# A two-layer transformer kernel: the eight row scatters of two batches, four in a row and two couples before, are given eight release points spread over two batches

## The chip, the cores and the metric

One core of a Trainium2 chip runs the whole program. The metric is device time in microseconds (us), lower is better. Engines are named as in the profile: PE is TensorE (matmul and transpose), DVE is VectorE, ACT is ScalarE, POOL is GpSimd, SP is SyncE, which here only issues transfers.

## The reference

Two transformer layers work on 32 batches of 256 rows of 128 features.

```
x  = L0_attn_x                                   # 32 x 256 x 128
xn = layernorm(x)
x  = x + attention0(xn) + moe0(xn)                # 16 heads, relative position bias clipped at 64
xn = layernorm(x)
x  = x + attention1(xn) + moe1(xn)                # ALiBi, causal; 16 experts with a capacity

# inside moe1
logits = xn @ router_w.T + router_b
vals, idx = top_k(logits, 2)
pos  = running count of each expert's rows        # in row order
slot = idx * capacity + pos                       # rows over the capacity are dropped
buf  = zeros(16 * capacity + 1, 128).at[slot].set(each row, twice)
h    = gelu(buf @ w1 + b1) @ w2 + b2              # then gathered back and weighted
```

The change concerns the line `buf = ... .at[slot].set(...)`: each normalized row is written twice, into the slots of its two experts. In the kernel `buf` is the DRAM tensor `packed`.

## The kernel before

The program has four stages one after the other: the first mixture of experts (0 to about 440 us of the trace), the first attention (about 440 to 1650), the second mixture's experts (to about 1945), and the second attention. The change is in the first attention.

The first attention takes the batches one by one, with eight steps for each batch (`UB = 8`): a step is 128 query rows times four heads. Step n belongs to batch b = n // 8 and has place r = n % 8; this document writes r0 to r7. In a step the four engines work on different ages of the data, by orders written out by hand:

- PE computes `score(n+1)` and `relative(n+5)` (lines 1172 and 1182), transposes the probabilities of step n-2 (`turn`, line 1194), and multiplies them with the values of step n-3 (line 1214) and with the relative table (lines 1229 and 1159). `score(n+1)` may start only when DVE has read the scores of step n (the semaphore `lowest`) and has copied the relative part (`rel_moved`).
- DVE adds scores and bias and takes the minimum, four instructions in a step (line 1013, tile `neg_scores`), each of which raises `lowest` by one; then it copies the relative part (`rel_s`, line 1021) and does small work that depends on r.
- ACT takes the exponentials (line 873) and moves the transposed probabilities out of PSUM (lines 889, 895).
- SP issues the transfers of the relative bias, a write to and a read from DRAM in each step (lines 764, 777).
- POOL makes the heads of the queries of the next batch (`query_heads`, line 825, or 828 for the later batches), and issues the scatters.

As soon as two batches of the first attention are complete, their 512 rows (a pair p, four tiles of 128 rows) are normalized, routed and counted, by small DVE work in the steps of the batches 2p+3 to 2p+5. In r5 of the odd batch b = 2p+5 DVE finishes the slots (`slots`, last instruction on line 985, semaphore `slots_done`). POOL then makes the row numbers (`rows_of(p)`, lines 816 and 818) and issues eight indirect DMAs, for each of the four tiles one to the first and one to the second expert (line 844). Each writes 128 rows of 512 bytes into `packed`. Sixteen pairs make 128 scatters. Batches 32 to 35 of this stage are already those of the second attention (ALiBi instead of the relative bias, shorter steps); the pairs 13, 14 and 15 are scattered at batches 31, 33 and 35.

A scatter has a release point: POOL waits until `lowest` has reached four times a step number, that is, until DVE has read all scores before that step. Before the change the eight of a pair wait, two by two, for the steps 8b+6, 8b+7, 8b+8 and 8b+9, capped at step 256 (`NU0`), beyond which no pacing exists. POOL works strictly in its order: what stands behind a scatter waits with it. Two things wait for the scatters to land: `rows_of(p+1)` (the list `scat` is reused) and the DVE normalization of pair p+2 (`normal_end`, r7 of an odd batch; the tile `xn2` is reused).

Of the kernel before, what the change touches and what calls it, by code (L numbers as in the profile page):

```python
# [61 lines left out]
def program(nc, io, nb, cap):  # L62
# [5 lines left out]
    with ctx:  # L68
# [7 lines left out]
        packed = nc.dram_tensor("packed", (SLOTS + 2 * T, D), F32).ap()  # L76
# [38 lines left out]
        with ExitStack() as pa:  # L115
# [10 lines left out]
            TP = 4  # L126
# [468 lines left out]
        with ExitStack() as pm:  # L595
# [9 lines left out]
            TP = 4  # L605
            UB = 8
            NU0 = UB * nb
            NB0 = nb + LATE
            NUL = UB * NB0
# [25 lines left out]
            xn2 = [sm(f"xn2_{i}", [P, TP, D]) for i in range(2)]  # L635
# [26 lines left out]
            scat = sm("scat", [P, TP, 2], U32)  # L662
# [12 lines left out]
            lowest = semm("lowest_ready")  # L675
# [18 lines left out]
            scattered = semm("scattered")  # L694
# [27 lines left out]
            for s in range(0, UB * (NB0 + 2)):  # L722
                b, r = divmod(s, UB)
                odd = b % 2 == 1
# [83 lines left out]
            @block.gpsimd  # L808
            def _(pool):
                for i in range(3):  # L810
                    pool.memset(bias[0][i][:, :, :], 0.0).then_inc(bias_zeroed, 1)
                def rows_of(p):
                    pool.wait_ge(slots_done, p + 1)
                    if p >= 1:
                        pool.wait_ge(scattered, 128 * p)
                    pool.tensor_tensor(scat_f[:, :, :], dumpk[:, :, :], sk[:, :, :], ALU.add).then_inc(rows_known, 1)
                    pool.wait_ge(rows_known, 2 * p + 1)
                    pool.tensor_copy(scat[:, :, :], scat_f[:, :, :]).then_inc(rows_known, 1)
                    pool.wait_ge(rows_known, 2 * p + 2)

                def query_heads(b):
                    pool.wait_ge(spare_free, job_no["q", b])
                    for i in range(4):
                        if b < nb:
                            ins = pool.tensor_scalar(q_of[b % 2][:, i, :], q_raw[:, :], cview["head_scale"][:, i:i + 1], q_bias[:, i:i + 1],  # L825
                                                     ALU.mult, ALU.add)
                        else:
                            ins = pool.tensor_scalar(q_of[b % 2][:, i, :], q_raw[:, :], cview["head_scale"][:, i:i + 1], None, ALU.mult)
                    ins.then_inc(q_ready, 1)

                query_heads(0)
                for b in range(nb + 5):
                    if b + 1 < NB0:
                        query_heads(b + 1)
                    if b == 2:
                        for h in range(H):
                            pool.tensor_scalar(alibi[:, h, :], cview["distance"], float(SLOPES[h]), None, ALU.mult).then_inc(alibi_built, 1)
                    p, odd = divmod(b - 5, 2)
                    if odd == 0 and 0 <= p < nb // 2:
                        rows_of(p)  # L840
                        for i in range(TP):
                            for k in range(2):
                                pool.wait_ge(lowest, 4 * min(NU0, UB * b + 6 + i))
                                pool.indirect_dma_start(
                                    out=packed, out_offset=bass.IndirectOffsetOnAxis(ap=scat[:, i, k:k + 1], axis=0),
                                    in_=xn2[p % 2][:, i, :], in_offset=None).then_inc(scattered, 16)
                pool.wait_ge(scattered, 128 * (nb // 2))

            @block.scalar
# [686 lines left out]
        with ExitStack() as pb:  # L1536
# [38 lines left out]
            lowest = semb("lowest_ready")  # L1575
# [16 lines left out]
            UB = 8  # L1592
# [353 lines left out]
```

## Time and profile before

| | |
|---|---|
| device time, three runs | 2600.22 us median (2595.81 to 2603.77) |
| the profiled execution | 2601.3 us, of which the span of the trace is 2599.2 us |
| busy share over the span | PE 87%, PEld (weight loads) 69%, DVE 74%, ACT 66%, POOL 32% |
| granted TensorE clock, mean | 0.951 |
| the 128 scatters (line 844) | 953 / 967 / 1207 ns on POOL (min / median / max), 625.9 to 1637.5 us |
| from a scatter's issue to its landing | 3.8 / 4.0 / 15.7 us |

All times are those of one profiled execution, counted from the span's start. The shares are averages over four stages with different limits; for this change the reader has to look at single steps of the first attention. In rows of the timeline the first number is the start, the second the duration, and the bracket at the end says how long the engine stood idle before the instruction and what released it; "issue" stands for an idle time in which the engine waited for nothing that the profile shows. Such a bracket is absent where the idle time was very short.

### The profile page before, as it was taken

To read this page: it belongs to the slowest core of one execution; us is meant where nothing else is said; L and a number is where in the kernel's file an instruction comes from. 1 tells how busy PE (TensorE), PEld (TensorE's weight loads), DVE (VectorE), ACT (ScalarE), POOL (GpSimd) and SP (SyncE) were. 2 spreads that over 40 slices of the span, in tenths; PEclk is the share of its full clock that TensorE was granted. 3 is DMA by queue.
4 is the path that set the end of the run, shared out by engine and by line. 5 is a ranking of instruction groups with operands and counts; after the bars stand their busy time and mean duration, and the time that the engine had idled before them with its cause. 6 is when DMAs were issued, how large, how long until landed. Compare 5 with 4: busy or idle time off the path is not lost. (4 is left out here: it accounts for less than half of the span.)

```text
span 2599.2 us, 86943 instructions
## 1 busy us (share of the span) xinstructions
PE 2248.8 (87%) x32420; PEld 1793.8 (69%) x32420; DVE 1927.7 (74%) x7683; ACT 1720.2 (66%) x5582; POOL 839.4 (32%) x906
## 2 busy tenths in 40 slices
PE   5999998898898898888888888799987888787888
PEld 4888886677777777777777765577775555555555
DVE  6877773787788877778878766588876767676777
ACT  2333332887677777777777778566656778777778
POOL 3566664021111111111111122212126444545451
PEclk9999998999999999999999999799998989999999
DMA  6867543776677766667767630222311110111110
GB/s 199 238 171 191 116 107 78 183 182 166 168 175 173 179 167 170 167 167 176 175 167 177 166 85 14 89 101 101 113 63 30 27 30 25 26 26 32 26 31 11
DMA packets 361046, 304.53 MB, mean 117 GB/s; under 512 B 25656, under 2 KB 329144, under 8 KB 359240
## 3 DMA queue, kind: packets, MB, share of 16 engines
q1 hardware_dynamic: 350152, 271.93, 41.2%
q0 software_dynamic: 10496, 27.28, 3.5%
q8 instruction: 252, 4.13, 0.7%
q14 instruction: 146, 1.20, 0.2%
HBM read 166.43 MB, written 132.69 MB: 115 GB/s over the span
## 5 line engine op out<-in xcount | busy, mean ns | idle before, releaser
L873 ACT ACTIVATE probs<-neg_scores,low 128x256 f32<-128x256 f32 (+1 forms) x1152 | 574.1, 501 | 147.7 <-DVE low L1013 119.3
L1013 DVE CUSTOM_DVE_ANT_0 neg_scores<-scores,rel_bias 128x256 f32<-128x256 f32 x1024 | 373.3, 421 | 186.4 <-PE scores L1182 134.8
L1773 DVE CUSTOM_DVE_ANT_0 neg_scores<-scores,alibi 128x128 f32<-128x128 f32 (+1 forms) x896 | 266.2, 353 | 129.4 <-remote 71.9
L1194 PE MATMUL probsT<-consts,probs 128*128 128x128 f32 x2240 | 321.3, 287 | 5.0 <-issue 2.7
L1172 PE MATMUL scores<-k_heads,q_heads 32*128 32x256 f32 (+1 forms) x2304 | 211.0, 432 | 101.3 <-DVE rel_s L1021 67.0
L1735 ACT ACTIVATE probs<-neg_scores,low 128x128 f32<-128x128 f32 (+1 forms) x448 | 199.8, 447 | 139.1 <-DVE low L1773 125.1
L1194 PEld LDWEIGHTS probsT<-consts,probs 128*128 128x128 f32 x2240 | 250.1, 145 | 38.2 <-issue 12.4
L889 ACT COPY probsT_s<-probsT 128x512 f32<-128x512 f32 x288 | 167.5, 582 | 151.6 <-PE probsT L1194 137.7
L295 POOL TENSOR_TENSOR hid<-hid,gate_bc 128x512 f32<-128x512 f32 x160 | 205.6, 1290 | 155.6 <-DVE hid L487 142.9
L825 POOL TENSOR_SCALAR q_heads<-q_raw,consts,q_bias 128x256 f32<-128x256 f32 x128 | 69.7, 560 | 551.2 <-ACT q_raw L856 551.1
L1021 DVE COPY rel_s<-scores 128x768 f32<-128x768 f32 x256 | 244.1, 953 | 3.9 <-DMA rel_rows<-rel_s 2.7
L324 ACT ACTIVATE ga<-gate_up 128x512 f32<-128x512 f32 x160 | 95.7, 598 | 227.2 <-PE gate_up L566 225.5
L1829 PE MATMUL scores<-rel_v 32*128 32x128 f32 (+1 forms) x1792 | 146.8, 399 | 94.1 <-DVE low L1773 80.6
L1841 PE MATMUL probsT<-consts,probs 128*128 128x128 f32 x1344 | 199.5, 287 | 23.9 <-DVE probsT_s L1781 20.9
L873 ACT ACTIVATION_READ_ACCUMULATOR probs<-neg_scores,low 128x1 f32 x1152 | 220.1, 191 | 0.0
L1172 PEld LDWEIGHTS scores<-k_heads,q_heads 32*128 32x128 f32 x2304 | 99.7, 189 | 165.3 <-issue 87.9
L1841 PEld LDWEIGHTS probsT<-consts,probs 128*128 128x128 f32 x1344 | 156.4, 147 | 62.0 <-issue 42.8
L1747 ACT ACTIVATE probs<-neg_scores,low 128x128 f32<-128x128 f32 (+1 forms) x448 | 198.5, 445 | 0.0
L1214 PE MATMUL values<-probsT_s,v_heads 128*32 128x128 f32 x4480 | 190.6, 286 | 3.7 <-issue 3.6
L1781 DVE COPY probsT_s<-probsT 128x512 f32<-128x512 f32 x224 | 154.0, 687 | 42.4 <-PE probsT L1841 25.3
L1829 PEld LDWEIGHTS scores<-rel_v 32*128 32x128 f32 x1792 | 76.5, 198 | 146.8 <-DVE low L1773 108.8
L577 PEld LDWEIGHTS ffn_down<-weights,hid 128*128 128x128 f32 x1280 | 167.1, 191 | 13.2
(227 smaller groups left out, 5132.3 us busy)
## 6 DMA issues: line engine op xcount, KB each, us to landing
rel_rows<-rel_s SPq DMA_DIRECT2D x256, 192.0 KB
rel_bias<-rel_rows SPq DMA_DIRECT2D x256, 192.0 KB, 3.4
gate_bc<-gate_rows SPq DMA_DIRECT2D x32, 1024.0 KB, 10.2
rel_rows<-rel_s SPq DMA_DIRECT2D x256, 128.0 KB
rel_bias<-rel_rows SPq DMA_DIRECT2D x256, 128.0 KB, 3.4
packed<-ffn_in SPq DMA_DIRECT2D x8, 1280.0 KB, 15.5
xe<-packed SPq DMA_DIRECT2D x16, 640.0 KB, 3.9
expert_out<-ye POOLq DMA_DIRECT2D x16, 640.0 KB, 3.2
```

Source lines behind the costliest of these rows:

```text
L295: pool.tensor_tensor(hid[p % 2][:, k, :], hid[p % 2][:, k, :], gate_bc[p % 2][:, min(k, NCHUNK), :], ALU.mult).then_inc(hid_done, 1)
L873: act.activation(probs[s % 3][:, j, 0:w], neg[s % 2][:, j, 0:w], ACT.Exp, bias=low[s % 3][:, j:j + 1], scale=-1.0, accum_out=sums[s // UB ...
L1013: dve.tensor_tensor_reduce(neg[s % 2][:, j, 0:w], S_ps[:, 512 * j:512 * j + w], bias_of(s)[:, j, :] if s < NU0 else alibi[:, 4 * j + s % 4 ...
L1021: dve.tensor_copy(rel_s[u % 2][:, :, :], S_ps[:, :].rearrange("p (j w) -> p j w", j=4)[:, :, S:S + 3 * R]).then_inc(rel_moved, 1)
L1172: ins = pe.matmul(S_ps[:, 512 * j:512 * j + w], q_of[b % 2][rows, i, qt * P:(qt + 1) * P], k_of[b % 2][rows, 0:w], start=True, stop=True)
L1194: ins = pe.transpose(PT_ps[kt][:, j * P:(j + 1) * P], probs[u % 3][:, j, kt * P:(kt + 1) * P], ident)
L1214: ins = pe.matmul(O_ps[rows, 0:P], v_of[b % 2][:, kt, i, rows], probsT[:, qt, i, kt, j, :], start=(i == 0 and kt == 0), stop=(i == 3 and k ...
L1735: act.activation(probs[s % 3][:, j, 0:w], neg[s % 3][:, j, 0:w], ACT.Exp, bias=low[s % 3][:, j:j + 1], scale=-1.0, accum_out=sums[g % 2][: ...
L1747: act.activation(probs[s % 3][:, j, 0:w], neg[s % 3][:, j, 0:w], ACT.Exp, bias=low[s % 3][:, j:j + 1], scale=-1.0, accum_out=sums[g % 2][: ...
L1773: dve.tensor_tensor_reduce(neg[s % 3][:, j, 0:w], S_ps[j][:, 0:w], alibi[:, 4 * j + i, S - w:S], 1.0, 3e38, ALU.add, ALU.min, low[s % 3][: ...
L1829: ins = pe.matmul(S_ps[j][:, 0:w], q_of[b % 2][rows, i, q0:q0 + P], kT[b % 2][rows, 0:w], start=True, stop=True)
L1841: ins = pe.transpose(PT_ps[kt][:, j * P:(j + 1) * P], probs[u % 3][:, j, kt * P:(kt + 1) * P], ident)
```

## The change

The eight scatters of a pair now have one release point each, spread over two batches, and the cap is the last step of the stage (288, `NUL`) instead of 256. With b the odd batch in which the slots are known, the places are: two scatters at 8b+7 and 8b+8; three in the next batch at its r3, r5 and r7; three in the batch after it at its r2, r3 and r5, ahead of that batch's `rows_of`. The last pair's last six have no release point.

```diff
+                def scatter(p, first, steps):
+                    for n, step in enumerate(steps):
+                        i, k = divmod(first + n, 2)
+                        if step is not None:
+                            pool.wait_ge(lowest, 4 * min(NUL, step))
+                        pool.indirect_dma_start(
+                            out=packed, out_offset=bass.IndirectOffsetOnAxis(ap=scat[:, i, k:k + 1], axis=0),
+                            in_=xn2[p % 2][:, i, :], in_offset=None).then_inc(scattered, 16)
+
                 query_heads(0)
                 for b in range(nb + 5):
                     if b + 1 < NB0:
...
+                    if b >= 7 and b % 2 == 1:
+                        scatter((b - 7) // 2, 5, [UB * b + r for r in (2, 3, 5)])
                     p, odd = divmod(b - 5, 2)
                     if odd == 0 and 0 <= p < nb // 2:
                         rows_of(p)
-                        for i in range(TP):
-                            for k in range(2):
-                                pool.wait_ge(lowest, 4 * min(NU0, UB * b + 6 + i))
-                                pool.indirect_dma_start(
-                                    out=packed, out_offset=bass.IndirectOffsetOnAxis(ap=scat[:, i, k:k + 1], axis=0),
-                                    in_=xn2[p % 2][:, i, :], in_offset=None).then_inc(scattered, 16)
+                        scatter(p, 0, [UB * b + 7, UB * b + 8])
+                    if odd == 1 and 0 <= p < nb // 2:
+                        scatter(p, 2, [UB * b + r for r in (3, 5, 7)] if b < nb + 4 else 6 * [None])
                 pool.wait_ge(scattered, 128 * (nb // 2))
```

Only POOL's order changes. Here is its row for two neighbouring pairs in the first attention before the change; `L825` is `query_heads`, four instructions for a batch, and `L816`, `L818` are `rows_of`.

```order
L816 TENSOR_TENSOR scat_f<-dumpk,sk 128x8
L818 CAST scat<-scat_f 128x8
L844 DMA packed<-xn_0,scat 36864x128 x8
L825 TENSOR_SCALAR q_heads<-q_raw,consts,q_bias 128x256 x8
L816 TENSOR_TENSOR scat_f<-dumpk,sk 128x8
L818 CAST scat<-scat_f 128x8
L844 DMA packed<-xn_1,scat 36864x128 x8
```

All eight scatters of a pair stand in one block, and the query heads of two batches follow it. The same place of POOL's row after the change, where the scatters have line 836:

```order
L816 TENSOR_TENSOR scat_f<-dumpk,sk 128x8
L818 CAST scat<-scat_f 128x8
L836 DMA packed<-xn_1,scat 36864x128 x2
L825 TENSOR_SCALAR q_heads<-q_raw,consts,q_bias 128x256 x4
L836 DMA packed<-xn_1,scat 36864x128 x3
L825 TENSOR_SCALAR q_heads<-q_raw,consts,q_bias 128x256 x4
L836 DMA packed<-xn_1,scat 36864x128 x3
L816 TENSOR_TENSOR scat_f<-dumpk,sk 128x8
L818 CAST scat<-scat_f 128x8
L836 DMA packed<-xn_0,scat 36864x128 x2
```

Three of a pair's scatters now stand behind the query heads of the next batch, and three behind those of the batch after it and ahead of the next pair's `rows_of`. The number of scatters, their size and every other instruction are as before.

## Rows read from the trace of the kernel before

**Rows 1.** The page, its first line.

```profile
span 2599.2 us, 86943 instructions
```

**Rows 2.** Timeline of DVE: first score instruction of steps 19 r0, r1, 20 r0, r1, r2.

```profile
1087.40 0.42 DVE L1013 CUSTOM_DVE_ANT_0 neg_scores<-scores,rel_bias 128x256 f32<-128x256 f32 x1 [0.61 <-ACT probs L873]
...
1091.22 0.42 DVE L1013 CUSTOM_DVE_ANT_0 neg_scores<-scores,rel_bias 128x256 f32<-128x256 f32 x1
...
1125.47 0.42 DVE L1013 CUSTOM_DVE_ANT_0 neg_scores<-scores,rel_bias 128x256 f32<-128x256 f32 x1 [2.80 <-PE scores L1182]
...
1130.28 0.42 DVE L1013 CUSTOM_DVE_ANT_0 neg_scores<-scores,rel_bias 128x256 f32<-128x256 f32 x1 [1.03 <-ACT probs L873]
...
1133.85 0.42 DVE L1013 CUSTOM_DVE_ANT_0 neg_scores<-scores,rel_bias 128x256 f32<-128x256 f32 x1 [1.24 <-PE scores L1182]
```

**Rows 3.** Windows, odd batches 5 to 29, r6 to the next r1: PE, PEld, DVE, ACT, POOL.

```profile
1111.15:1130.28 19.13, 14.29 (x291) 11.02 (x293) 12.04 (x52) 9.22 (x30) 8.22 (x10) 0.82 0.52 129
...
1180.49:1197.14 16.65, 11.48 (x294) 9.10 (x293) 11.85 (x52) 9.33 (x30) 8.14 (x10) 1.00 0.59 147
...
sum 242.81, PE 177.77 PEld 138.91 DVE 155.64 ACT 119.47 POOL 106.67; mean PE 13.67 PEld 10.69 DVE 11.97 ACT 9.19 POOL 8.21
```

**Rows 4.** The same three steps of even batches 6 to 30, same columns.

```profile
1148.27:1160.55 12.28, 11.25 (x311) 9.86 (x311) 11.12 (x53) 9.24 (x32) 0.00 (x0) 1.00 0.77 190
...
sum 160.64, PE 147.28 PEld 129.09 DVE 144.66 ACT 120.61 POOL 0.00; mean PE 11.33 PEld 9.93 DVE 11.13 ACT 9.28 POOL 0.00
```

**Rows 5.** Waits of PE, 1111.15 to 1131, then 1131 to 1180.4: total, times, longest.

```profile
PE projected L1159 <- issue: 2.8, 5, 1.1
...
PE scores L1172 <- DVE rel_s L1021: 2.3, 6, 0.8
```

**Rows 6.** Timeline of POOL, pair 7, batches 19 and 20.

```profile
1112.24 1.05 POOL L844 DMA_INDIRECT packed<-xn,scat  x1 [0.53 <-POOL scat L818]
...
1116.14 0.97 POOL L844 DMA_INDIRECT packed<-xn,scat  x1 [0.30 <-issue]
...
1127.21 0.96 POOL L844 DMA_INDIRECT packed<-xn,scat  x1 [6.48 <-DVE low L1013]
1128.48 0.97 POOL L844 DMA_INDIRECT packed<-xn,scat  x1 [0.30 <-issue]
```

**Rows 7.** Line 844 alone: what POOL waited for before it: total, times.

```profile
  issue: 26.0, 85
```

**Rows 8.** Timeline of DVE, batches 31 to 34: waits during pairs 13 and 14.

```profile
1532.12 0.29 DVE L1030 COPY ctx_s<-values 128x128 f32<-128x128 f32 x1 [7.24 <-issue]
...
1536.03 0.29 DVE L1013 CUSTOM_DVE_ANT_0 neg_scores<-scores,alibi 128x128 f32<-128x128 f32 x1 [2.00 <-PE scores L1172]
...
1592.16 0.42 DVE L1075 TENSOR_TENSOR ctxT<-ctx_s,projected 128x256 f32<-128x256 f32 x1 [6.91 <-remote]
```

**Rows 9.** Timeline, batch 33 r6 and r7, pair 14: a scatter that stood alone.

```profile
1578.67 1.06 POOL L844 DMA_INDIRECT packed<-xn,scat  x1 [0.53 <-POOL scat L818]
...
1580.08 1.25 PE L1194 MATMUL probsT<-consts,probs 128*128 128x128 f32 x8
...
1581.12 0.42 DVE L1013 CUSTOM_DVE_ANT_0 neg_scores<-scores,alibi 128x256 f32<-128x256 f32 x1
...
1582.82 0.97 POOL L844 DMA_INDIRECT packed<-xn,scat  x1 [3.09 <-DVE low L1013]
```

**Rows 10.** Timeline, batch 15: start of r2 on DVE; query heads of batch 16.

```profile
954.93 0.42 DVE L1013 CUSTOM_DVE_ANT_0 neg_scores<-scores,rel_bias 128x256 f32<-128x256 f32 x1 [1.24 <-PE scores L1182]
...
955.83 2.18 POOL L825 TENSOR_SCALAR q_heads<-q_raw,consts,q_bias 128x256 f32<-128x256 f32 x4 [28.55 <-ACT q_raw L856]
```

**Rows 11.** Window, batch 19 r1 to r5, columns as before.

```profile
1091.22:1111.15 19.93, 18.43 (x406) 15.62 (x402) 17.48 (x76) 16.93 (x55) 2.18 (x4) 1.00 0.76 183
```

**Rows 12.** Timeline, end of the stage: last scatter of pair 15, next stage.

```profile
1637.45 0.95 POOL L844 DMA_INDIRECT packed<-xn,scat  x1 [0.30 <-issue]
1650.59 1.84 POOL L1524 MEMSET v_heads<- 128x1024 f32 x2 [12.18 <-POOLq L595]
```

## The prediction

> **What bounds the kernel now.** The span is 2599.2 us [rows 1]; the profiled execution took 2601.3, which is 1.1 above the median of the three runs. The sum below is made against 2601.3 and 1 us is taken off at its end. The page only says that PE is busiest, so I went to the timeline of the first attention and cut it at the first score instruction of each step.
>
> An undisturbed step is a loop of two engines: DVE reads four score banks and copies the relative part, PE computes the next scores, DVE goes on. It shows between r1 and r2 of batch 20: 1130.28 to 1133.85, 3.57 us, with a wait of DVE for PE's scores of 1.24 [rows 2]. ACT, SP and POOL have room.
>
> Then I compared the same three steps (r6, r7 and the next batch's r0) in odd batches, where scatters run, and in even ones, where none does, by a table of windows. Thirteen odd ones take 242.81 us, 18.68 each [rows 3]; thirteen even ones take 160.64, 12.36 each [rows 4]. DVE's busy time is 11.97 against 11.13, so the odd ones have 0.84 us more work on DVE; that cannot make 6.32. PE executes fewer instructions there and is still busy longer, at a granted clock that in most of these windows is 0.8 and in the even ones 1.00.
>
> What is late is PE. In the first window of batch 19 it stands idle five times, 2.8 us together, for "issue", which means for nothing that the profile shows; in the next 49 us, without scatters, it waits only for DVE [rows 5]. The pauses lie beside the scatters: four are issued one after the other from 1112.24 to 1116.14, and after the couple of 1127.21 and 1128.48 DVE resumes 1.80 us behind the second issue [rows 2, 6]. Of the 128 scatters, 85 are issued 0.3 us after another [rows 7]. So I read it thus: scatters close upon each other hold PE up, until about 1.8 us after the last of them is issued, and through PE the loop.
>
> **The change, part by part.** Nothing is added or removed in work: 128 scatters of about 0.96 us on POOL, the same bytes, the same `rows_of` and query heads. What changes is the company of each scatter.
>
> (1) Removed, main part. The thirteen pairs 0 to 12 lose the burst of four and both couples. An odd window without them should take between 12.36 (its extra DVE work hidden) and 13.20 (not hidden); I take 12.8, since the loop leaves DVE idle time in some of the steps only. The excess is 18.68 less 12.8, 5.9 us, times 13: 76 us; with the bounds 71 to 82.
>
> (2) Removed, batches 31 to 34. Past step 256 the scatters were not paced. During pair 13 DVE idles 7.24 and 2.00 us, during pair 14 6.91 [rows 8]; of each some 1 to 2 may be there without scatters, as the ordinary step waits 1.24 [rows 2]. I count 8 and 5, together 13 us, bounds 9 to 16.
>
> (3) Added, a scatter alone. In the even batches r3, r5, r7 and in the odd ones r5, r7 and the following r0. The upper bound is a full couple: r0 of batch 20 takes 4.81 us (1125.47 to 1130.28), r0 of batch 19, with none, 3.82 (1087.40 to 1091.22), so 0.99 for two, 0.5 for each if it is shared [rows 2]. The lower bound is zero, and the only scatter in this stage that stood alone speaks for it: issued at 1578.67, the next one at 1582.82; PE's transposes at 1580.08 start without a pause and take 1.25 us, and DVE begins r7 at 1581.12 without a wait [rows 9]. That step had slack on DVE, so it is no proof. But geometry helps too: a release point lies at the end of DVE's four score instructions, the issue 0.3 us behind; a hold that ends 1.8 us behind the issue ends just when the next scores are due, since of the 3.57 us of a step about 2.1 are left behind the four. I take 0.05 each, six to a pair: 0.3.
>
> (4) Added, a couple that the table of release points does not show. In the odd batches two release points, r2 and r3, stand behind the query heads. These are made from 955.83 to 958.01, while r2 starts at 954.93 and its four score instructions are through about 1.5 us later [rows 10]. Both release points have passed when POOL is free, and the two scatters go 1.27 us apart, as before. Such a couple costs 0 to 0.99. It falls ahead of r3 to r5, in which DVE has small work: the five steps r1 to r5 take 19.93 [rows 11] against five times 3.57, so some 2 us in which a late PE is partly hidden. I take 0.4. With (3) that is 0.7 a pair, 9 us over 13; bounds 0 to 13 times (6 times 0.5 and 0.99), 52.
>
> (5) Added, late. In the batches 32 to 34 the steps take 2 to 3 us and the query heads 3.8, so the release points r3 and r5 of an even batch, and r2, r3 and r5 of batch 33, come together: two couples and a triple. I take 4 us, bounds 0 to 8.
>
> (6) The last pair. Its last six are unpaced and start one step later than before, when the burst of eight ended at 1637.45 and the stage at 1650.59 [rows 12]. The last issue moves from 1637.45 to about 1639.4; the burst is shorter. I take 1 us of loss, bounds a gain of 2 and a loss of 2.
>
> What else is moved past something: the query heads have nothing new ahead of them when they are due, as the scatter before them (r7 of the even batch, or step 8b+8) is issued a step or more earlier than ACT's copy, for which POOL idled 28.55 us [rows 10]. `rows_of` of the next pair waits for the landing of a scatter that is released at the end of r4's scores; 4.0 us to land ends inside r5, before DVE has the slots. `normal_end` comes two steps later. SP's transfers are in another queue; DVE waits for PE, not for a transfer, in the rows above. I cost all of these at nothing; a late `rows_of` would shift scatters only.
>
> Sum: 76 + 13 - 9 - 4 - 1 = 75 us. 2601.3 - 75 = 2526, and on the median's scale 2525.
>
> **A rule weighed against the rows.** The scatters run while PE pauses, and not in the windows without [rows 3 to 6]. The Trainium skill, SBUF — State Buffer, section "SBUF: two separate sides", has engine ports and DMA ports apart, so that "A DMA cannot be slowed by a compute op, and vice versa". By that rule PE's pauses could not be the transfers' doing, and moving them would gain nothing; the time would be 2600. The rows disagree as far as coincidence can.
>
> **The rivals.**
>
> A. A scatter alone costs half a couple, 0.5, and the new couple its 0.99: (3) and (4) become 4.0 a pair, 52 us. 76 + 13 - 52 - 4 - 1 = 32: 2568. For it: the stage's one lone scatter had slack. Against it: a burst of four costs more than two couples, which speaks for a cost of nearness.
>
> B, the other side. What counts is the number of separate holds, not their sum: each scatter alone, close behind the release, holds the next scores up as long as a couple does, 0.99. Eight holds a pair are 7.9 us against 5.9 now, a loss of 2 times 13, 26 us; late pairs break even. That is 2626. It decides from a price of 0.73 (5.9 / 8) upwards. For it: even steps have no slack, while the old place in r6 and r7 had DVE's small work to hide in. Against it: the lone scatter [rows 9], and that DVE resumes at a fixed distance behind the last issue, which for a lone one is 1.27 us earlier.
>
> C. PE's pauses are not due to the scatters but to what else odd batches do in r6 and r7 (many short matmuls of line 1159, which even batches also have without pausing [rows 4]). Then nothing changes: 2600.
>
> D. Not only the pauses but the clock recovers further than counted, and both new prices are zero: 82 + 16 + 2 = 100, 2501.
>
> **How the numbers follow.** The forecast with its bounds (2506 to 2556) has 0.70, A 0.13, B 0.06, C 0.04, D 0.04; 0.03 is left for what I don't see. The range 2506 to 2562 leaves out B, C, D and most of A, two in ten. A measurement here can tell 0.3% (8 us) from no change. Faster: forecast, A, D and part of the rest, 0.89; within 0.3%: C and a mild B, 0.04; slower: 0.07.
>
> **What would show it.** In the changed kernel the three steps from r6 of odd batches should take about 13 us at a granted clock near 1.00, and PE's "issue" pauses at lines 1159 and 1229 should be gone. (3) is right if the even steps r3, r5 and r7 keep 3.6 us or their own length; under A or B they are 0.5 to 1 longer. (4) is right if two issues stand 1.27 us apart at the end of each odd r2 and r3 to r5 lengthen by less than 0.5 together. (6) shows in the end of the stage relative to the last score step. Wrong would be: a wait of DVE for `scattered`, or of PE for the query heads.

## The result and the profile after

The changed kernel takes 2527.53 us (median of four runs, 2525.11 to 2531.41), the kernel before 2601.99 beside it (four runs, 2595.81 to 2617.08): ratio 0.9707, 95% interval 0.9663 to 0.9751. The forecast was 2525, range 2506 to 2562. The profiled execution took 2531.41 us; its span is 2529.6 against 2599.2 before [rows 1], 69.6 less, and the mean granted clock is 0.964 against 0.951. Lines behind the edit have moved down by 8: DVE's scores are L1021, PE's second values line is L1237, the scatters are L836.

The tables below show windows of the trace: start and end, length, then busy time and count of PE, PEld, DVE, ACT and POOL, granted clock, DMA share and GB/s. First the three steps r6, r7 and the next r0 of the odd batches 5 to 29 after the change, which answer to [rows 3]:

```profile
1147.98:1160.41 12.43, 9.43 (x268) 7.96 (x270) 11.77 (x52) 8.55 (x28) 2.35 (x4) 1.00 0.66 155
...
1277.35:1290.24 12.89, 11.01 (x269) 9.31 (x270) 11.96 (x51) 8.33 (x28) 2.36 (x4) 0.87 0.62 154
...
sum 163.75, PE 130.35 PEld 110.03 DVE 153.72 ACT 109.97 POOL 30.84; mean PE 10.03 PEld 8.46 DVE 11.82 ACT 8.46 POOL 2.37
```

242.81 has become 163.75: 79.1 us are gone, 12.60 a window are left. The same three steps of the even batches, which now hold a lone scatter each, answer to [rows 4]:

```profile
sum 160.40, PE 147.04 PEld 128.91 DVE 144.65 ACT 120.19 POOL 12.54; mean PE 11.31 PEld 9.92 DVE 11.13 ACT 9.25 POOL 0.96
```

160.64 before, 160.40 after: the lone scatter in each of them, released when r6's scores are read and issued 1.7 us into that step, costs nothing. The loss is in the steps r1 to r5. First the odd batches, which answer to [rows 11]; batch 5 has no scatters there, batch 21 has the new couple and one lone scatter:

```profile
609.29:629.22 19.93, 18.44 (x406) 15.63 (x402) 17.47 (x76) 16.93 (x55) 2.17 (x4) 1.00 0.76 187
...
1126.42:1147.98 21.56, 19.13 (x406) 15.95 (x402) 17.58 (x76) 16.81 (x55) 5.12 (x7) 1.00 0.73 179
...
sum 278.26, PE 248.32 PEld 206.83 DVE 228.38 ACT 218.62 POOL 63.51; mean PE 19.10 PEld 15.91 DVE 17.57 ACT 16.82 POOL 4.89
```

Then r1 to r5 of the even batches:

```profile
1095.76:1114.14 18.38, 17.59 (x364) 14.63 (x364) 13.82 (x54) 16.58 (x54) 4.16 (x6) 1.00 0.77 194
...
sum 239.00, PE 228.82 PEld 190.05 DVE 179.57 ACT 214.03 POOL 53.94; mean PE 17.60 PEld 14.62 DVE 13.81 ACT 16.46 POOL 4.15
```

An odd one with the couple is 1.63 longer than one without; an even one is 18.38 where the same steps took 17.99 before the change, without a scatter in them. In the even batches it is the scatter with the release point r3, which opens with r2's last score instruction, 1.5 us into r2: POOL is still making the query heads, and the scatter is issued 3.24 us into r2 instead of 1.74. The timeline of batch 20 shows the issue, the start of r3 and a pause of PE; this r2 takes 4.05 us and not 3.67:

```profile
1102.57 1.03 POOL L836 DMA_INDIRECT packed<-xn,scat  x1 [0.16 <-issue]
...
1103.40 0.42 DVE L1021 CUSTOM_DVE_ANT_0 neg_scores<-scores,rel_bias 128x256 f32<-128x256 f32 x1 [1.06 <-issue]
...
1103.99 0.32 PE L1237 MATMUL values<-probsT_s,rel_v 128*32 128x64 f32 x5 [0.33 <-issue]
```

In the odd batches two scatters follow the query heads, 1.33 us apart, and PE pauses three times in r3. In batch 21 r2 takes 4.07 us where it took 3.68 before, and r3 5.16 where it took 3.94: 0.39 for the late first scatter, 1.22 for the second:

```profile
1133.23 1.02 POOL L836 DMA_INDIRECT packed<-xn,scat  x1 [0.16 <-issue]
...
1134.56 0.97 POOL L836 DMA_INDIRECT packed<-xn,scat  x1 [0.30 <-issue]
1134.70 0.27 PE L1237 MATMUL values<-probsT_s,rel_v 128*32 128x64 f32 x2 [0.39 <-issue]
...
1135.45 0.27 PE L1237 MATMUL values<-probsT_s,rel_v 128*32 128x64 f32 x2 [0.48 <-issue]
...
1136.20 0.28 PE L1237 MATMUL values<-probsT_s,rel_v 128*32 128x64 f32 x2 [0.47 <-issue]
```

The end of the stage answers to [rows 12]: the last pair's burst, in which DVE waits 5.63 us for PE, and the next stage's first POOL instruction:

```profile
1573.72 0.97 POOL L836 DMA_INDIRECT packed<-xn,scat  x1 [0.30 <-issue]
1576.46 0.42 DVE L1088 TENSOR_TENSOR residual<-residual,projected 128x256 f32<-128x256 f32 x1 [5.63 <-PE projected L1138]
1583.03 1.84 POOL L1532 MEMSET v_heads<- 128x1024 f32 x2 [8.34 <-POOLq L595]
```

From r1 of batch 31 to that MEMSET the kernel before took 149.4 us (1501.15 to 1650.59), this one 132.3 (1450.70 to 1583.03): 17.1 less. Most of it is in two places, r7 of batch 31 and r0 of batch 34, whose windows before the change are these:

```profile
1523.42:1536.03 12.61, 7.10 (x77) 4.67 (x81) 3.27 (x17) 2.23 (x8) 5.51 (x6) 0.64 0.11 36
1584.32:1592.94 8.62, 4.86 (x38) 3.02 (x39) 1.35 (x11) 3.10 (x12) 5.53 (x6) 0.74 0.16 54
```

By the first score instruction of each step in the two timelines, r7 of batch 31 and r0 of batch 32 together went from 16.96 us to 6.25, and r0 of batch 34 from 8.61 to 1.55: 17.8 less. The other steps of the batches 31 to 35 grew by 2.6, and the stretch from the stage's last step to that MEMSET shrank by 1.9.

### The profile page after: what moved, and what is told of

Same layout as the page of the kernel before. It is cut to its first block and busy times, and to the rows that moved or that the text cites. A ratio compares the mean times of both kernels' runs of the same rounds, so it can differ in the third digit from the quotient of the medians.

```text
span 2529.6 us, 86943 instructions
## 1 busy us (share of the span) xinstructions
PE 2213.3 (87%) x32420; PEld 1774.4 (70%) x32420; DVE 1928.9 (76%) x7683; ACT 1714.5 (68%) x5582; POOL 839.1 (33%) x906
## 5 line engine op out<-in xcount | busy, mean ns | idle before, releaser
L1021 DVE CUSTOM_DVE_ANT_0 neg_scores<-scores,rel_bias 128x256 f32<-128x256 f32 x1024 | 373.2, 421 | 151.7 <-PE scores L1190 102.2
L1202 PE MATMUL probsT<-consts,probs 128*128 128x128 f32 x2240 | 312.1, 282 | 2.3 <-ACT probsT_s L897 1.0
L1202 PEld LDWEIGHTS probsT<-consts,probs 128*128 128x128 f32 x2240 | 242.3, 142 | 34.4 <-issue 5.0
L836 POOL DMA_INDIRECT packed<-xn,scat x128 | 126.0, 984 | 325.6 <-DVE low L1021 310.9
L1849 PE MATMUL probsT<-consts,probs 128*128 128x128 f32 x1344 | 201.4, 289 | 23.2 <-DVE probsT_s L1789 19.9
L825 POOL TENSOR_SCALAR q_heads<-q_raw,consts,q_bias 128x256 f32<-128x256 f32 x128 | 69.1, 551 | 438.6 <-ACT q_raw L864 438.5
L1849 PEld LDWEIGHTS probsT<-consts,probs 128*128 128x128 f32 x1344 | 157.9, 148 | 62.1 <-issue 42.3
```

The lines of the kernel that those rows point to most:

```text
L1021: dve.tensor_tensor_reduce(neg[s % 2][:, j, 0:w], S_ps[:, 512 * j:512 * j + w], bias_of(s)[:, j, :] if s < NU0 else alibi[:, 4 * j + s % 4 ...
L1202: ins = pe.transpose(PT_ps[kt][:, j * P:(j + 1) * P], probs[u % 3][:, j, kt * P:(kt + 1) * P], ident)
L1849: ins = pe.transpose(PT_ps[kt][:, j * P:(j + 1) * P], probs[u % 3][:, j, kt * P:(kt + 1) * P], ident)
```

## The experiments

The kernels are told by the groups in which they ran, because a group shares a chip, and the kernel before ran beside each on the same chip. Which chip it was turned out to matter more than anything that I had meant to try. In what follows, "a chip with the hold" is one on which the kernel before takes 2600 us, and a quick one takes 2386. PE is held where it pauses beside scatters and the steps grow longer.

**Other places (e1 to e4, one chip).** e1_all_alone gives each of the eight a release point of its own, none of them behind the query heads:

```diff
-                        scatter((b - 7) // 2, 5, [UB * b + r for r in (2, 3, 5)])
+                        scatter((b - 7) // 2, 6, [UB * b + r for r in (4, 5)])
...
-                        scatter(p, 2, [UB * b + r for r in (3, 5, 7)] if b < nb + 4 else 6 * [None])
+                        scatter(p, 2, [UB * b + r for r in (4, 5, 6, 7)] if b < nb + 4 else 6 * [None])
```

> The changed kernel with other release points: in the even batch r4, r5, r6 and r7, in the odd batch after it r4 and r5, so that POOL is free of query heads at each and every scatter of the batches up to 31 goes alone, 0.3 us behind its release. Theory H (a scatter delays PE only in a stretch at a fixed distance behind its issue; if that stretch ends before the next scores are due, it is free): the couples at odd r2 and r3 (1.6 us in each of 12 pairs, from the windows r1 to r5 of 21.5 against 19.9) and the late lone scatter of the even batches (0.39 us, windows of 18.4 against 18.0) both go, 19 + 5 = 24 us: about 2503. All r1 to r5 windows are back at 19.9 and 18.0. Rival N (each scatter that is issued in a step without slack costs some tenths of a us wherever it lies): the cost only moves, as many scatters lie in tight steps as before; 2520 to 2528.

e2_even_r4 moves only the even r3 scatter to r4 (`(4, 5, 7)` for `(3, 5, 7)`).

> The changed kernel with one release point moved: the even batch's r3 becomes r4, so that this scatter no longer follows the query heads (3.2 us into r2) but lies 0.3 us behind the scores of r3. Theory H: even r2 goes from 4.05 back to 3.67, 13 times 0.39 = 5 us, about 2522; the odd batches don't change. Rival N: the 0.39 us turns up in r3 or r4 instead, 2527, no change.

e3_no_scatters is the kernel before without its 128 scatters and the waits for them; the rows that they would pack are missing from the result.

> The kernel before without its 128 scatters and without the waits for them (the second mixture of experts then works on rows that were never written); row numbers are still made. It is the floor of every placing. Theory H: below the changed kernel by the 24 us of couples and late scatters, and by what batches 31 to 35 and the last burst still pay (some 5 to 12): 2492 to 2498; odd r6 to r0 about 12.4 to 12.6, so that the lone scatters in those steps prove to be free. Rival N: lower still, by at least 0.2 us for each of about 90 lone scatters, 18 us: 2475 to 2480.

e4_late_paced is the kernel before with one word changed, the cap of the release points:

```diff
-                                pool.wait_ge(lowest, 4 * min(NU0, UB * b + 6 + i))
+                                pool.wait_ge(lowest, 4 * min(NUL, UB * b + 6 + i))
```

> The kernel before with one edit, the cap of the release points at step 288 instead of 256: only the pairs 13 to 15 (batches 31 to 35) are paced, in couples. It prices term (2) of the prediction by itself. Theory H: pair 13 gets the cost of a middle pair (about 6 us in place of 9), pair 14 little, pair 15 a little later: 3 to 6 us faster, about 2597. If the unpaced bursts cost more than their waits show, more than 8 us; if pacing in couples only moves the cost, nothing (2602).

On their chip the kernel before takes 2385.81 us (31 runs, 2382.39 to 2389.92), and nothing moves it: all alone 2387.15, ratio 1.0013 [1.0004, 1.0023]; even r4 2388.17, 1.0006 [0.9997, 1.0016]; no scatters at all 2383.48, 0.9988 [0.9979, 0.9998]; paced late 2387.18, 1.0006 [0.9996, 1.0016] (one of its ten runs took 11171.12 us; the ratio leaves it out). An expectation that counts from 2600 us is off by over 100 for that reason, and no theory on the places was tested. What e4 did show is the windows of [rows 3] again, with bursts and couples as before the change:

```profile
626.68:639.16 12.48, 10.10 (x268) 8.21 (x270) 11.82 (x52) 8.36 (x28) 7.95 (x10) 1.00 0.70 180
...
sum 163.72, PE 134.03 PEld 112.55 DVE 153.72 ACT 110.04 POOL 103.32; mean PE 10.31 PEld 8.66 DVE 11.82 ACT 8.46 POOL 7.95
```

The ten POOL instructions with their burst of scatters are there (7.95 us a window), and the sum is 163.72 where the pair's chip gave 242.81. It is the sum that the changed kernel has, and e3, without any scatter, has 163.4 in these steps. So on this chip these scatters don't lengthen the steps.

**One profile with many placings.** To price placings side by side, whatever the chip, e5_mixed gives each pair a list of its own, (kind, step counted from the batch of its slots):

```diff
+            ALONE = (7, 8, 12, 13, 14, 15, 20, 21)
+            COUPLES = (8, 8, 12, 12, 14, 14, 21, 21)
+            BURST = (12,) * 8
+            OLD = (6, 6, 7, 7, 8, 8, 9, 9)
+            NEW = (7, 8, 11, 13, 15, 18, 19, 21)
...
+                        if rel < 90:
+                            pool.wait_ge(lowest, 4 * min(NUL, UB * (2 * p + 5) + rel))
```

One pair's scatters are left out, another's move half the rows, and two pairs' rows go to other places by ordinary transfers. e6_alone_again is e1's kernel beside it.

> One kernel with another placing for each pair, read step by step. Pairs 0 and 6: all alone, 0.3 us behind a release, in the odd batch r6 and r7, in the even one r3 to r6, in the next odd one r3 and r4. Pairs 1 and 12: four couples. Pair 2: eight in a row at r3 of the even batch. Pairs 3 and 9: alone, but behind a delay of three or six small memsets. Pair 4: the old places, with plain instead of indirect transfers by POOL, into the rows for dropped tokens. Pair 5: the same transfers issued by SP. Pair 7: the old places. Pairs 8, 13, 14, 15: the new places. Pair 10: no scatters. Pair 11: the old places, each scatter with 64 rows instead of 128 (so the rows of pairs 4, 5, 10 and half of 11 are not delivered). Theory H on a chip that shows the delay: pair 0 costs under 0.3 us against pair 10, a couple 1.0 to 1.6, the eight in a row about 9, a lone scatter that is issued 0.7 to 1.5 us behind the release 0.3 to 0.8 in each tight step, plain transfers by POOL as much as indirect ones, SP's nothing. If it is the bytes and not the issue, SP's cost as much as POOL's and the half ones half. On a chip without the delay, as in the four runs before, every placing costs under 0.2 us a pair; then the difference between the chips, not the placing, is what the measured gain depends on.

> The kernel of the first experiment once more, because the runs of that group came from a chip on which the kernel before takes 2386 us instead of 2600, in which no placing mattered. If this chip takes 2600 for the kernel before: theory H says 2503, rival N 2520 to 2528, as before. If it takes 2386: no difference.

Another chip, on which the kernel before takes 2386.13 us (13 runs). e5 took 2394.77 (one run); the 9 us more lie at the end of the stage, where 21.3 us pass between the last step and the next stage's first POOL instruction (11.5 in e4), for a reason that I did not follow. e6 took 2388.17, ratio 1.0006 [0.9996, 1.0015]. In e5 the steps don't know which pair they serve: between the odd batches 7 and 29 no r6 or r7 differs by more than 0.5 us from that of another pair.

**The same kernel elsewhere, and twice the scatters.** e7_after_elsewhere is the changed kernel itself. e8_twins is the kernel before with a second scatter behind each:

```diff
+                                pool.indirect_dma_start(
+                                    out=packed_twin, out_offset=bass.IndirectOffsetOnAxis(ap=scat[:, i, k:k + 1], axis=0),
+                                    in_=xn2[p % 2][:, i, :], in_offset=None).then_inc(scattered, 16)
```

> The changed kernel itself, beside the kernel before, on whatever chip these runs get. Theory H: the hold of PE behind scatters belongs to the chip on which the pair was first measured, where the kernel before takes 2600 us; on a chip where it takes 2386 there is no hold and nothing to gain. There: ratio 0.999 to 1.001, 2384 to 2389 us, r6 to r0 of the odd batches 12.6 us in both kernels. Should the kernel before take about 2600 here, 2525 to 2533. Rival N: the gain belongs to the kernel, through something that the experiments' variants changed away. Then the ratio is 0.97 here too, about 2316 beside 2386.

> The kernel before, with each scatter issued twice: the second one, right behind, writes the same rows to a tensor that nobody reads. 16 scatters to a pair where 8 were, in bursts of 8, 4 and 4. Theory H on a chip without the hold: PE is not held by any number; the 8 more are 7.7 us of POOL a pair and are hidden, 2384 to 2394 us. Theory S (the hold is there on every chip, and eight scatters are merely too few to show): some of the loop's steps r6 to r0 grow beyond 4.8, 4.1 and 3.9 us, 2 to 6 us a pair, 2415 to 2480. On a chip with the hold: 5.9 us a pair now, at least as much again for the twins, 2680 to 2720 beside 2600.

> The changed kernel with another placing or kind of scatter for each pair, so that one profile prices them side by side: all eight alone (pairs 0, 6), four couples (1, 12), a burst of eight (2), alone behind a wait of POOL (3, 9), ordinary transfers issued by POOL (4) and by SP (5) in the old places, the old places (7), the new ones (8, 13, 14), none (10), half the rows in the old places (11), six at the end (15). On a chip where the kernel before takes 2386 us: every odd r6 to r0 takes 12.6 to 12.7 us and every even r2 3.68, whatever the pair, total 2390 to 2397. On a chip where it takes 2600: old places 18.7 us for r6 to r0, burst of eight 9 or more over 12.6 at the odd r4 to r7, even r2 4.05 for the new places and 3.67 for all alone; half the rows tells whether bytes or issues count, SP's whether the queue matters.

A third chip of this kind, the kernel before at 2386.55 us (13 runs). The changed kernel takes 2387.91, ratio 1.0006 [0.9997, 1.0016]: as theory H said, and N, by which the gain belongs to the kernel, is out. Its windows in the order used above, r6 to r0 of odd batches, then r1 to r5 of odd, then r1 to r5 of even ones:

```profile
sum 163.54, PE 130.01 PEld 110.09 DVE 153.53 ACT 109.78 POOL 30.86; mean PE 10.00 PEld 8.47 DVE 11.81 ACT 8.44 POOL 2.37
```

```profile
sum 259.21, PE 239.77 PEld 203.11 DVE 227.34 ACT 219.16 POOL 63.53; mean PE 18.44 PEld 15.62 DVE 17.49 ACT 16.86 POOL 4.89
```

```profile
sum 233.87, PE 226.00 PEld 188.85 DVE 179.60 ACT 214.26 POOL 54.01; mean PE 17.38 PEld 14.53 DVE 13.82 ACT 16.48 POOL 4.15
```

I take these as the steps without a hold, as e3 without any scatter has the same lengths within 0.4 us a sum. Against them the pair's trace of the changed kernel has 0.2, 19.1 and 5.1 us too much, 24.4 together; that of the kernel before has 79.3 too much in the first and nothing in the others (259.19 and 233.88).

e8 took 2414.45 us (one run), 28 more than before: more than H allowed (2394), and next to the lower end of theory S (2415), by which the hold is there on every chip. Its trace, laid beside e4's (29.8 us longer), divides this. About 11 us lie between the stage's last step and the next stage's first POOL instruction, behind the last pair's sixteen scatters. 6.6 lie in r3 and r4 of the even batches, where POOL is late: with sixteen scatters to a pair, 1.27 us apart where they are not paced, the query heads of the next batch come late, and DVE stands 3.57 us for PE's scores at r4 of batch 20:

```profile
1098.76 1.62 POOL L826 TENSOR_SCALAR q_heads<-q_raw,consts,q_bias 128x256 f32<-128x256 f32 x3
...
1101.11 0.42 DVE L1017 CUSTOM_DVE_ANT_0 neg_scores<-scores,rel_bias 128x256 f32<-128x256 f32 x1 [3.57 <-PE scores L1186]
```

This was forgotten in the expectation. The third part is r0 of the even batches, in which three or four scatters are issued: it is 0.65 us longer in the mean, 8.4 together. In six of these thirteen steps PE has short pauses for "issue", up to 0.29 us, which none of the same steps of e4 has. Batch 16 shows one:

```profile
956.27 1.29 PE L1163 MATMUL projected<-z,consts 128*32 128x64 f32 x43 [0.29 <-issue]
```

So a weak form of theory S is not excluded: denser scatters may hold PE a little on a quick chip too. No run separates that from what a late POOL does to r0. e9, the mixed kernel, took 2397.89, again with 21.3 us at the end of the stage.

**The mixed kernel a third time, and then on a chip with the hold.** e10 is e5's kernel once more; e11_phases has every scatter in place and other placings for some pairs, among them lone scatters behind three or six small POOL instructions, which delay the issue by 0.8 and 1.6 us:

```diff
+            HOLES = (7, 8, 11, 13, 15, 20, 21, 21)
...
-                    plan("plain", OLD), plan("sp", OLD), plan("rows", ALONE), plan("rows", OLD),
-                    plan("rows", NEW), plan("wait2", ALONE), plan("none", ALONE), plan("half", OLD),
+                    plan("wait2", ALONE), plan("rows", HOLES), plan("rows", ALONE), plan("rows", OLD),
+                    plan("rows", NEW), plan("wait1", NEW), plan("wait2", NEW), plan("rows", ALONE),
```

> The mixed kernel once more, for the case that its chip is one where the kernel before takes 2600 us: it leaves out the scatters of one pair and half the rows of another, and writes two pairs' rows to other places. On such a chip: old places 18.7 us for the odd r6 to r0, the burst of eight 9 or more over 12.6, even r2 4.05 for the new places against 3.67 where all stand alone at a release. Theory Q (the queue matters): SP's pair and the pair without scatters have 12.6, the pair with half the rows as much as the whole one. Theory Y (the bytes matter): half the rows half the excess, SP's pair the same excess as POOL's. On a chip where the kernel before takes 2386: 12.6 for all, 2390 to 2398.

> Every scatter is made, in another place for each pair: alone at the even r4 to r7 and odd r4 and r5 (pairs 0, 6, 11), the same a little later behind three or six small instructions of POOL (3 and 4), four couples (1, 12), a burst of eight (2), the places before the change (7), those after it (8, 13, 14) and those a little later (9, 10), a mix (5), six at the end (15). Theory H, on a chip where the kernel before takes 2386 us: no step knows where the scatters are; every odd r6 to r0 12.6 to 12.7 us, every even r2 3.68, every odd r1 to r5 19.9 to 20.0; total 2385 to 2392. On a chip where it takes 2600: 18.7 for pair 7's r6 to r0, over 21 for pair 2's steps with the burst, even r2 4.05 for pairs 8, 13, 14 and 3.67 for 0, 6, 11; the later ones tell whether a lone scatter has a dear and a cheap phase.

e10 met a fourth chip of the quick kind: 2397.28 us, the kernel before 2385.87. e11 at last met a chip on which the kernel before takes 2599.93 (one run each), and took 2521.61 there. The two have the same burst of eight from r3 of batch 10 on (pair 2) and the same two couples in r3 and r5 of batch 8 (pair 1). Windows of r1 to r5 of batches 8, 10 and 12 in e10, where there is no hold:

```profile
705.04:723.03 17.99, 17.39 (x364) 14.53 (x364) 13.81 (x53) 16.50 (x54) 5.68 (x8) 1.00 0.76 190
767.91:785.90 17.99, 17.39 (x364) 14.53 (x365) 13.81 (x53) 15.85 (x53) 9.02 (x12) 1.00 0.85 209
831.18:849.17 17.99, 17.38 (x364) 14.52 (x363) 13.81 (x53) 16.57 (x54) 6.97 (x16) 1.00 0.78 197
```

The windows of e11, batches 8, 10, 12, 14 and 18: two couples; eight in a burst; three alone, 0.8 us late; three alone, 1.6 us late; three alone, each at its release (pair 6). The sixth row is batch 22 with the places of the changed kernel (pair 8):

```profile
702.52:722.84 20.32, 18.51 (x390) 15.32 (x387) 13.81 (x53) 17.41 (x56) 6.11 (x8) 1.00 0.78 191
768.32:795.91 27.59, 21.11 (x364) 16.67 (x364) 14.00 (x53) 16.54 (x54) 10.02 (x12) 0.88 0.57 145
841.01:860.20 19.19, 17.79 (x382) 14.94 (x382) 13.82 (x53) 17.29 (x56) 7.00 (x16) 1.00 0.78 191
905.96:925.08 19.12, 18.04 (x380) 15.09 (x379) 13.98 (x54) 17.17 (x56) 8.49 (x25) 1.00 0.76 187
1035.07:1053.06 17.99, 17.39 (x364) 14.54 (x364) 13.82 (x54) 16.39 (x54) 5.15 (x7) 1.00 0.79 202
1164.70:1183.76 19.06, 17.63 (x364) 14.64 (x364) 13.81 (x53) 16.39 (x54) 4.16 (x6) 1.00 0.77 188
```

The prices follow by taking 17.99 away. A couple costs 1.17 (2.33 for two), eight in a row 9.60. A lone scatter at its release costs 0.00; delayed by 0.8 us it costs 0.40 and by 1.6 us 0.38. So in a couple the first scatter is free if it is issued at its release, and the second holds the loop up by about 1.2 us. In the burst that would be seven holds of 1.37; part of it may be the clock, which is at 0.88 there and at 1.00 in the other rows. The price of a late lone scatter isn't fixed: in batch 22 the one behind the query heads costs 1.07, issued 3.26 us into r2, where the pair's trace has 0.39 for the same place (4.05 had been expected for this r2, 4.75 were measured), and one that is issued 0.4 us into r3 of batch 24 costs 0.84. The list of PE's waits during the burst (total, times, longest) has ten pauses:

```profile
PE values L1292 <- issue: 5.3, 8, 1.2
PE probsT L1257 <- issue: 0.6, 2, 0.3
```

This fits the kernel before in the mean, and not window by window. For each pair it has a burst of four and two couples, in which three, one and one scatters are not the first: 5 times 1.20 is 6.0, and 6.10 were measured (79.3 / 13). But its thirteen windows lie between 3.5 and 8.4 over 12.60: five of them from 16.12 to 17.08 us, eight from 19.13 to 21.03. Pair 7 of e11, in the same old places, is of the shorter kind, 16.69 where 18.7 had been expected:

```profile
1085.28:1101.97 16.69, 13.30 (x293) 10.75 (x293) 11.86 (x52) 9.33 (x30) 8.19 (x10) 0.80 0.60 146
```

In the eight long ones it is mostly r7 that is long, 8.7 to 10.5 us against 4.06. In batch 19 the granted clock is at its lower level, 1.2 GHz, for 3.4 us within that r7. What makes a window of one kind or the other is open. For the new couple of the changed kernel, a late first scatter (0.39) and a second one (1.20) are 1.59, and 12 times 1.59 is the 19.1 that were measured; the two prices show one by one in r2 and r3 of batch 21 above.

The timeline of batch 18 shows a lone scatter of r3 at its release; r4 starts 3.58 us behind r3, which is the undisturbed length:

```profile
1042.32 0.42 DVE L1076 CUSTOM_DVE_ANT_0 neg_scores<-scores,rel_bias 128x256 f32<-128x256 f32 x1 [0.68 <-DVE residual L1143]
...
1044.07 1.03 POOL L889 DMA_INDIRECT packed<-xn,scat  x1 [2.32 <-DVE low L1076]
1045.90 0.42 DVE L1076 CUSTOM_DVE_ANT_0 neg_scores<-scores,rel_bias 128x256 f32<-128x256 f32 x1 [0.46 <-PE scores L1245]
```

The same step of batch 12 with the issue 0.8 us later takes 3.97, and DVE waits 0.85:

```profile
850.80 1.03 POOL L889 DMA_INDIRECT packed<-xn,scat  x1 [0.28 <-POOL scratch L878]
852.24 0.42 DVE L1076 CUSTOM_DVE_ANT_0 neg_scores<-scores,rel_bias 128x256 f32<-128x256 f32 x1 [0.85 <-PE scores L1245]
```

**All alone, a last time.** e12 is e1's kernel, sent in the hope of a chip with the hold.

> All eight alone, in every pair (8b+7, 8b+8, even r4 to r7, odd r4 and r5). From the steps of the run before: on a chip where the kernel before takes 2600 us, thirteen times the new couple (1.47) and the scatter behind the query heads (0.39) go, 24 us less than the changed kernel's 2528: 2504, bounds 2499 to 2510, ratio 0.963. On a chip where it takes 2386: 2385 to 2389, ratio 1.000 to 1.002.

It met a fifth chip of the quick kind: 2386.98 us, ratio 1.0006 [0.9997, 1.0016]. On a chip with the hold this placing has been seen pair by pair in e11 (pairs 0, 6 and 11: r1 to r5 take 17.99 and 19.93 or 19.94, and r6 to r0 what they take on quick chips), but was never timed as a whole. By the steps it would be 24 us quicker than the changed kernel; that is an estimate from the 19.1 and 5.1 above.

## Why the prediction was right, and where it wasn't

The forecast of 75 us less met 74.5 (medians) and 69.6 (spans). The mechanism was right for the main term: on this chip scatters close upon each other hold PE up. That the sum came out within 1 us was luck, because errors of about 15 and 12 us cancelled, and it holds for one kind of chip only: on the quick chip of e7 the same change gave nothing (ratio 1.0006), which neither the forecast nor its bounds allowed for.

**(1), burst and couples.** 76 forecast, 79.1 measured [rows 3]. Of the right size: without the hold a window takes 12.60, not 12.8. What makes up its 6.1 us is less well known. In the thirteen odd windows of the kernel before, PE's pauses for "issue" at the lines 1159 and 1229 (over 0.15 us each) are 76 and make 38.9 us together, half of the 79. The sign that they would be gone came true in r6 to r0, where none is left; in r1 to r5 the new couples and late scatters bring 46, 19.4 us together.

**(2), (5), (6), the late batches.** 13, less 4, less 1: 8 forecast, 17.1 measured. I had priced their waits by what DVE idled in a few places [rows 8], 13 us; the unpaced scatters cost more than those, 17.8 in the steps named above. The new couples and the triple of (5) cost 2.6 of the 4 expected, if all that the other steps grew by is theirs. (6) had the wrong sign: the end is 1.9 us shorter and not 1 longer.

**(3), a scatter alone.** 0.05 each was near for five of the six: the steps in which they are issued keep their length. The sixth, with the release point r3 of an even batch, isn't free: it stands behind the query heads and costs 0.39, 5.1 us in all. I had seen this for the odd batches and put the even one among those that are issued at their release.

**(4), the new couple.** 0.4 forecast with 0.99 as the upper bound; 1.59 measured for each of the twelve, 19.1 in all. This is the term that failed. The cover that I counted on, DVE's small work in r3 to r5, is not there in r3 (5.16 us against 3.94), and e11's couple in r4 of batch 9 still costs 0.85; the bound was wrong too: it came from r0 of batch 20 [rows 2], a couple issued at the release, whose first scatter was free. One that starts 1.5 us late pays for both. With (3) that is 24.2 where I said 9. Of these 15 us (1) gave back 3 and the late batches 9; the three measured parts make 79.1 - 24.2 + 17.1 = 72.0, and the last 2.4 us to the spans' 69.6 lie outside them: the changed kernel's trace is 4.7 us behind already at r1 of batch 5, before any scatter, and gains 2.0 after the stage.

**Rival A** (half a couple for a lone one) is near for most scatters that are late, 0.40 against its 0.5, and wrong for one at the release. **Rival B** (a hold each, as dear as a couple) is out for scatters at their release, 0.00 against its 0.73; of the late ones two reach it, 0.84 and 1.07. **Rival C**, that pauses are not the scatters' doing, is wrong on such a chip: in e11 the burst was moved to a place where the steps have no other reason to grow, and PE's pauses and 9.60 us came with it. On the quick chip of e7 its time is the right one: no change. **D**, both prices zero, is near the estimate for a placing without scatters behind the query heads (2504), and not for this one.

**The rule of the Trainium skill**, SBUF — State Buffer, section "SBUF: two separate sides", that a DMA and a compute operation cannot slow each other: on the quick chips the runs agree with it nearly (128 scatters fewer, ratio 0.9988 [0.9979, 0.9998]; e8 has the short pauses told above); in the pair's own traces and in e11 compute does wait beside transfers. Whether that goes through SBUF at all no run here shows.

What stays open is what makes the two kinds of chip, and by what path a scatter holds PE: the profile says only "issue". The traces differ in nothing that I can find on POOL's side: a scatter takes 984 ns in the mean in the changed kernel's traces of both and lands in a median of 4.1 us, and the packets and bytes of each queue are the same. Each chip was met in one group of runs only, so these runs can't tell a property of the chip from something else that held while the group ran. That half the rows, ordinary transfers or SP's queue would hold PE less was never seen on a chip with the hold, since the pairs with them (e5, e9, e10) met the other kind three times.

## What to carry to other kernels

Time the kernel before on the chip of each experiment, and look at its own time first: 2386 or 2600 us tells here which effects can show at all. Where POOL issues transfers while PE and DVE pass work to each other in a tight loop, look for PE's pauses for "issue" beside them (0.2 to 1.2 us here), and space the transfers by a step of the loop with each right behind DVE's score reads; of a couple only the first was free here. An instruction behind a longer one on its queue isn't released where its wait says (3.24 us into r2 here, and not 1.74): read its issue time for every batch kind, even and odd.

## What was not expected of the hardware

The same kernel takes 2384.0 us of span on one chip and 2529.6 on another, with equal instructions. A row of each page, first the chip with the hold, then the other: DVE's scores of the second attention, where POOL gathers rows (the last figures are DVE's idle time ahead of the group and what ended most of it; "remote" is what the profile writes where it finds no instruction that released the engine).

```profile
L1781 DVE CUSTOM_DVE_ANT_0 neg_scores<-scores,alibi 128x128 f32<-128x128 f32 (+1 forms) x896 | 266.1, 353 | 128.0 <-remote 72.1
```

```profile
L1781 DVE CUSTOM_DVE_ANT_0 neg_scores<-scores,alibi 128x128 f32<-128x128 f32 (+1 forms) x896 | 266.1, 353 | 48.8 <-PE scores L1837 45.0
```

The gathers alone (112 of them, line 1657) show how long that part takes, from the first one's start to the last one's: 582.8 us against 475.0.

```profile
L1657 POOL DMA_INDIRECT expert_rows<-expert_out,slot_ids x112: 940/952/1056, 1881.1 to 2463.9; - x112
```

```profile
L1657 POOL DMA_INDIRECT expert_rows<-expert_out,slot_ids x112: 940/952/1053, 1848.0 to 2323.0; - x112
```

So 108 of the 146 us between the two chips lie there, over four times the 24.4 that the changed kernel still loses in the steps of the first attention, and pacing the gathers may be the larger prize on a chip with the hold. That they hold PE in the same way is read from the likeness only; no experiment moved a gather.
